# Seeding two score banks with ScalarE copies of the negated maxima, in place of a fourth product with ones

## The reference, cut to what matters

```
q = jnp.einsum('bnd,hde->bhne', query, Wq) * scale
k = jnp.einsum('bmd,hde->bhme', query, Wk)
v = jnp.einsum('bmd,hde->bhme', query, Wv)
logits = jnp.einsum('bhne,bhme->bhnm', q, k)
attn = jax.nn.softmax(logits, axis=-1)
out = jnp.einsum('bhnm,bhme->bnhe', attn, v)
...
return jnp.dot(out, Wp) + bp
```

## Time and profile before

| what | value |
|---|---|
| time, median of 3 runs | 1872.64 us (1872.44 to 1873.9) |
| span of the profiled execution, first to last instruction | 1867.0 us |
| median of the runs less that span | 5.6 us |
| PE busy | 1829.2 us, 98% |
| POOL busy | 1339.4 us, 72% |
| DVE busy | 1216.5 us, 65% |
| ACT busy | 856.0 us, 46% |

### The profile page before, as it was taken

One profiled execution on the slowest core, in us unless ns is written; L12 is line 12 of the kernel. 1 busy time (PEld: TensorE's weight loads), 2 busy tenths in 40 slices (PEclk: granted clock), 3 DMA queues, 4 the chain that ended last, 5 costly groups with the idle time before them and its releaser, 6 DMA issues.

```text
span 1867.0 us, 30732 instructions
## 1 busy us (share of the span) xinstructions
PE 1829.2 (98%) x11400; PEld 1163.7 (62%) x11400; DVE 1216.5 (65%) x2155; ACT 856.0 (46%) x1098; POOL 1339.4 (72%) x711
## 2 busy tenths in 40 slices
PE   7999999999999999999999999999999999999998
PEld 5555555555665555556666565556665555598887
DVE  6666666666666657766666657766666668765565
ACT  3444444444435443443345544443444534475775
POOL 2798778788767867788677767887668787652664
PEclk9999999999999999999999999999999999999999
DMA  4300000002211000022211000022111011453431
GB/s 118 128 24 18 24 18 24 18 24 85 91 46 46 24 18 24 21 81 87 70 45 42 18 7 24 24 80 65 50 39 42 18 35 35 125 159 106 161 136 35
DMA packets 132142, 104.24 MB, mean 56 GB/s; under 512 B 58140, under 2 KB 118684, under 8 KB 130972
## 3 DMA queue, kind: packets, MB, share of 16 engines
q1 hardware_dynamic: 128924, 93.81, 16.8%
q0 software_dynamic: 3072, 8.46, 1.3%
HBM read 69.15 MB, written 29.43 MB: 53 GB/s over the span
## 4 chain that ended last, share of the span: by engine, by line
PE 87%; DVE 4%; POOL 4%; issue 2%; ACT 2%; DMA 1%; SPq 0%; POOLq 0%; DVEq 0%; ACTq 0%
PE score_ps L1161 23%; PE av_ps L1177 23%; PE spare_ps L1123 9%; PE spare_ps L1139 8%; PE spare_ps L1116 4%; PE y_ps L1749 4%; PE spare_ps L441 4%; PE h_ps L1720 4%; PE spare_ps L1188 3%; POOL prob_sum L1037 3%; DVE max_of L1328 1%; PE spare_ps L490 1%; PE spare_ps L465 1%; PE score_ps L1123 0%; PE y_ps L441 0%
## 5 line engine op out<-in xcount | busy, mean ns | idle before, releaser
L1037 POOL TENSOR_TENSOR prob_sum<-prob_sum,probs 128x1024 f32<-128x1024 f32 (+1 forms) x384 | 907.3, 2363 | 196.7 <-ACT probs L1272 164.7
L1328 DVE TENSOR_REDUCE max_of<-spare_ps 128x1 f32<-128x512 f32 x1024 | 656.9, 683 | 336.1 <-PE spare_ps L1139 325.7
L1272 ACT ACTIVATE probs<-score_ps 128x1024 f32<-128x1024 f32 x512 | 502.6, 1026 | 664.4 <-PE score_ps L1161 653.0
L1177 PE MATMUL av_ps<-probs,v 128*64 128x512 f32 x2048 | 487.9, 602 | 2.2 <-ACT probs L1272 1.4
L1177 PEld LDWEIGHTS av_ps<-probs,v 128*64 128x64 f32 x2048 | 129.8, 136 | 240.3 <-issue 218.3
L1033 POOL TENSOR_TENSOR prob_sum<-probs 128x1024 f32<-128x1024 f32 (+1 forms) x64 | 150.4, 2350 | 144.2 <-ACT probs L1272 144.0
L1139 PE MATMUL spare_ps<-k_hi,q_hi 64*128 64x512 f32 x1024 | 227.9, 439 | 11.5 <-DVE max_of L1328 10.6
L1139 PEld LDWEIGHTS spare_ps<-k_hi,q_hi 64*128 64x128 f32 x1024 | 98.1, 184 | 213.1 <-issue 176.9
L1161 PE MATMUL score_ps<-q_hi,k_hi 64*128 64x512 f32 x1024 | 209.0, 403 | 0.2 <-ACT probs L1272 0.2
L1161 PE MATMUL score_ps<-shift_rows,ones 64*128 64x512 f32 x1024 | 203.5, 392 | 0.0
L1161 PE MATMUL score_ps<-q_lo,k_hi 64*128 64x512 f32 x1024 | 202.7, 391 | 0.0
(11 more groups left out here) (278 smaller groups left out, 2367.7 us busy)
## 6 DMA issues: line engine op xcount, KB each, us to landing
o_transposed<-o_out SPq DMA_DIRECT2D x64, 256.0 KB, 2.0
v<-in_L_ffn_W_dram SPq DMA_DIRECT2D x16, 1024.0 KB, 5.6
o_in<-o_transposed SPq DMA_DIRECT2D x28, 512.0 KB, 4.1
w_raw<-in_L_attn_Wq_dram SPq DMA_DIRECT2D x64, 64.0 KB, 2.3
w_raw<-in_L_attn_Wk_dram SPq DMA_DIRECT2D x64, 64.0 KB, 2.2
wv_raw<-in_L_attn_Wv_dram SPq DMA_DIRECT2D x32, 128.0 KB, 3.0
shift_rows<-neg_rows SPq DMA_DIRECT2D x256, 1.0 KB
x<-in_x_dram SPq DMA_DIRECT2D x4, 1024.0 KB, 5.9
```

What stands on the lines that cost most here:

```text
L1037: pool.tensor_tensor(out, out, probs[:, n % RING, heads], ALU.add).then_inc(prob_added, 1)
L1177: last = pe.matmul(av_ps[hd * E:(hd + 1) * E, :], v[:, quad % 2, kt, 2 * first_head + hd, :], probs[:, n % RING, hd, :], start=(kt == 0), ...
L1272: act.activation(probs[:, n % RING], score_ps[n % 2][:, :, :], ACT.Exp).then_inc(probs_ready, 1)
L1328: dve.tensor_reduce(max_of[:, u % 2, kh, j, hd:hd + 1], bank[:, :], AX.X, ALU.max).then_inc(pass_read, 1)
```

## The change

The fourth product goes for all scores but the first two. In its place ScalarE writes -max, as a full 128 x 1024 tile, into the score buffer before the score (the step "seed"), and the three products of q and k add to what stands there: their first matmul no longer starts a new sum. To have -max on all 128 partitions, SyncE moves it to a small tensor in DRAM (`shift_dram`) with four transfers, and then reads it back with one transfer of 512 KB that repeats it on every partition (`spread_shift` into `shift_all`, two buffers). Space for that comes from `o_out`: the normalised output is now written over `sums`, and `turn_sum` waits until the store of the unit before has landed. In the order of steps "seed seed" stands behind each pair of scores, scores now always come in pairs, and in the second line one av moved from the end to the middle.

```
-    "early av av av pass score score pass sum av recip pass score score pass late bite bite",
-    "bite norm score pass early av pass score score pass score pass late av av av",
-    "av pass score score pass early av sum pass score score pass bite late av recip av",
-    "pass norm score score pass early bite bite av pass score score pass late av av av"))
+    "early av av av pass score score seed seed pass sum av recip pass score score seed seed pass late bite bite",
+    "bite norm pass score score seed seed pass early av av pass score score seed seed pass late av av",
+    "av pass score score seed seed pass early av sum pass score score seed seed pass bite late av recip av",
+    "pass norm score score seed seed pass early bite bite av pass score score seed seed pass late av av av"))
...
+            if name == "seed" and h < HALVES and KT * u + kt + 2 < KT * UNITS:
+                yield "seed", KT * u + kt + 2
...
             def move_shift(u):
                 sp.wait_ge(max_done, u + 1)
-                wait(sp, score_ready, KT * (u - 1))
+                wait(sp, shift_in[u % 2], 16 * (u // 2))
                 for r in range(P // BLOCK):
                     rows = neg_rows[r * BLOCK:r * BLOCK + 2 * JT, :]
-                    heads = shift_rows[0:E + 1:E, u % 2, :].rearrange("h (j r i) -> h r j i", j=JT, i=BLOCK)
-                    sp.dma_start(heads[:, r].bitcast(F32), rows.bitcast(F32)).then_inc(shift_in[u % 2], 16)
+                    heads = shift_dram[u % 2].rearrange("h (j r i) -> h r j i", j=JT, i=BLOCK)
+                    sp.dma_start(heads[:, r], rows.bitcast(F32)).then_inc(shift_out, 16)
+
+            def spread_shift(u):
+                sp.wait_ge(shift_out, 64 * (u + 1))
+                wait(sp, seeded, KT * (u - 1) - 2)
+                sp.dma_start(shift_all[:, u % 2], shift_dram[u % 2].rearrange("(a h) n -> a h n", a=1)
+                             .broadcast_to([P, 2, BANK])).then_inc(shift_in[u % 2], 16)
...
-                wait(pe, probs_ready, n - 1)
+                products = [(k_hi[:, par, keys], q_hi[:, par, tokens]), (k_hi[:, par, keys], q_lo[:, par, tokens]),
+                            (k_lo[:, par, keys], q_hi[:, par, tokens])]
                 if n < 2:
+                    pe.wait_ge(first_shift, 64)
...
+                    products.append((one_rows[:, :], shift_rows))
+                else:
+                    pe.wait_ge(seeded, n - 1)
...
+                        last = pe.matmul(score_ps[n % 2][:, hd, :], a[rows], b[rows], start=(n < 2 and i == 0),
+                                         stop=(i == len(products) - 1), skip_group_check=n > 1)
...
+            def seed(n):
+
+                u, kt = divmod(n, KT)
+                if kt == 0 or n == 2:
+                    act.wait_ge(shift_in[u % 2], 16 * (u // 2 + 1))
+                act.wait_ge(probs_ready, n - 1)
+                act.activation(score_ps[n % 2][:, :, :], shift_all[:, u % 2], ACT.Copy).then_inc(seeded, 1)
...
             def turn_sum(u):
                 bank, = spare(("sum", u))
                 dve.wait_ge(sum_ready, u + 1)
-                wait(dve, o_done, u)
+                wait(dve, o_stored[(u - 1) % 2], 16 * ((u + 1) // 2))
                 dve.transpose(sums[:, :], bank[:, :]).then_inc(sum_turned, 1)
...
             def normalise(u):
                 dve.wait_ge(av_ready, KT * (u + 1))
                 dve.wait_ge(recip_spread, u + 1)
-                wait(dve, o_stored[u % 2], 16 * (u // 2))
-                dve.tensor_tensor(o_out[:, u % 2, :], av_ps[:, :], sums[:, :], ALU.mult).then_inc(o_done, 1)
+                dve.tensor_tensor(sums[:, :], av_ps[:, :], sums[:, :], ALU.mult).then_inc(o_done, 1)
```

More of the change, by code:

```diff
@@ L816, in build_attention @@
         neg_rows = sb("neg_rows", [P, BLOCK], F32R)
-        shift_rows = sb("shift_rows", [P, 2, BANK], F32R)
+        shift_all = sb("shift_all", [P, 2, 2, BANK])
+        shift_rows = route.o_hi[:, :, :].rearrange("p c n -> p (c n)")[:, 0:BANK]
         score_ps = [ctx.enter_context(nc.psum_tensor(f"score_ps{i}", [P, 2, BANK], F32)) for i in range(2)]
@@ L856, in build_attention @@
         max_found = sem("max_found")
+        first_shift = sem("first_shift")
+        shift_out = sem("shift_out")
         shift_in = [sem(f"shift_in{i}") for i in range(2)]
+        seeded = sem("seeded")
         score_ready = sem("score_ready")
@@ L905, in load_wv, with move_first_shift @@
                                  ).then_inc(wv_loaded, 16)
+            def move_first_shift():
+                sp.wait_ge(max_done, 1)
+                for r in range(P // BLOCK):
+                    rows = neg_rows[r * BLOCK:r * BLOCK + 2 * JT, :]
+                    heads = shift_rows[0:E + 1:E, :].rearrange("h (j r i) -> h r j i", j=JT, i=BLOCK)
+                    sp.dma_start(heads[:, r].bitcast(F32), rows.bitcast(F32)).then_inc(first_shift, 16)
             def move_shift(u):
                 sp.wait_ge(max_done, u + 1)
-                wait(sp, score_ready, KT * (u - 1))
+                wait(sp, shift_in[u % 2], 16 * (u // 2))
                 for r in range(P // BLOCK):
                     rows = neg_rows[r * BLOCK:r * BLOCK + 2 * JT, :]
-                    heads = shift_rows[0:E + 1:E, u % 2, :].rearrange("h (j r i) -> h r j i", j=JT, i=BLOCK)
-                    sp.dma_start(heads[:, r].bitcast(F32), rows.bitcast(F32)).then_inc(shift_in[u % 2], 16)
+                    heads = shift_dram[u % 2].rearrange("h (j r i) -> h r j i", j=JT, i=BLOCK)
[5 more added lines that the diff above has]
+                             .broadcast_to([P, 2, BANK])).then_inc(shift_in[u % 2], 16)
             def store_o(u):
@@ L917, in store_o @@
                 b, hp, c = u // (2 * PER_BATCH), u // 2 % PER_BATCH, u % 2
-                sp.dma_start(oT_dram[b, hp, :, c * BANK:(c + 1) * BANK], o_out[:, u % 2, :]
+                sp.dma_start(oT_dram[b, hp, :, c * BANK:(c + 1) * BANK], sums[:, :]
                              ).then_inc(o_stored[u % 2], 16)
@@ L951, in _ @@
             sp.wait_ge(rows_set, 2)
+            move_first_shift()
             move_shift(0)
+            spread_shift(0)
             for h in range(HALVES):
@@ L979, in _ @@
                     move_shift(u + 1)
+                    spread_shift(u + 1)
                 if h == 1:
@@ L1047, in _ @@
             pool.memset(prob_sum[:, 0, 0, 0:P], 1.0).then_inc(rows_zeroed, 1)
-            pool.memset(o_out[:, :, :], 0.0).then_inc(rows_zeroed, 1)
+            pool.memset(sums[:, :], 0.0).then_inc(rows_zeroed, 1)
             pool.wait_ge(rows_zeroed, 2)
             pool.tensor_copy(one_rows[:, :], prob_sum[:, 0, 0, 0:P]).then_inc(rows_set, 1)
-            pool.tensor_copy(shift_rows[:, :, :], o_out[:, :, :]).then_inc(rows_set, 1)
+            pool.tensor_copy(shift_rows, sums[:, :]).then_inc(rows_set, 1)
             pool.wait_ge(rows_set, 2)
@@ L1155, in score @@
                     pe.wait_ge(rows_set, 2)
-                products = ((k_hi[:, par, keys], q_hi[:, par, tokens]), (k_hi[:, par, keys], q_lo[:, par, tokens]),
-                            (k_lo[:, par, keys], q_hi[:, par, tokens]), (one_rows[:, :], shift_rows[:, u % 2, :]))
+                    products.append((one_rows[:, :], shift_rows))
+                else:
+                    pe.wait_ge(seeded, n - 1)
                 for i, (a, b) in enumerate(products):
@@ L1160, in score @@
                         rows = slice(hd * E, (hd + 1) * E)
-                        last = pe.matmul(score_ps[n % 2][:, hd, :], a[rows], b[rows],
-                                         start=(i == 0), stop=(i == len(products) - 1))
+                        last = pe.matmul(score_ps[n % 2][:, hd, :], a[rows], b[rows], start=(n < 2 and i == 0),
+                                         stop=(i == len(products) - 1), skip_group_check=n > 1)
                 last.then_inc(score_ready, 1)
@@ L1286, in _ @@
                     exp(*at)
+                if name == "seed":
+                    seed(*at)
                 if name == "wp":
@@ L1336, in read_pass @@
                     dve.wait_ge(max_found, u + 1)
-                    wait(dve, shift_in[(u - 1) % 2], 64 * ((u + 1) // 2))
+                    wait(dve, first_shift, 64 if u > 0 else 0)
+                    wait(dve, shift_out, 64 * u)
                     dve.transpose(neg_rows[:, :].bitcast(F32), neg_max[:, :].bitcast(F32)).then_inc(max_done, 1)
```

7 lines of the change are left out of this document (3 added, 4 removed).

## The result

The changed kernel takes 1840.3 us (1838.4 to 1841.4) against 1873.3 us (1872.4 to 1875.7) for the kernel before on the same chip: ratio 0.983, 95% interval 0.982 to 0.984. So 33 us are saved where 64 were forecast, and the time lies inside the range.

What follows compares the result with a forecast made beforehand. TensorE, busy 98% of the span, was taken to bound nearly every stretch of attention. 117 - 13 - 22 - 10 - 5 - 3 = 64 us saved gave 1808 us against a median of 1872.6, range 1775 to 1842.

Steps and rivals of the forecast that it cites:

- The price of 0.23 us for a product: TensorE's scores: a fourth product of two heads costs 0.23 us; 510 scores losing one save 117 us.
- The duration of a seed and its overlap: ScalarE: a seed takes 0.93 to 1.06 us; 0.93 behind another, 1.05 to its end.
- the order and VectorE: TensorE's passes wait for VectorE's maxima, as they come 0.46 us sooner behind each pair: 5 us more lost.
- The 3 for the ends: Maxima of the last two units late against their scores, and first seeds after two transfers in a row: 3 us lost.
- stalls of scores on seeds: TensorE's second scores wait for seeds in short gaps, and the q bite's pass for q_hi: 32 x 0.4 = 13 us lost.
- route work: ScalarE's norms and table loads stand behind seeds and delay four places in each of three sequences: 10 us lost, an estimate.
- 0.45 us late in each even unit: k bites' high parts behind seeds free the second bank at 6.6 us; the pass ahead of the scores wants it at 6.1.
- The 22 us: Even units: TensorE's sum waits for GpSimd's unbroken adds and weight split, 16.8 us; with bank losses in 12 units, 22 us lost.
- (b): Rival: ScalarE's chain heavier, seeds 1.06 us without overlap, three short gaps of four halves stall; 38 us more, about 1845; 14%.
- (a): Rival: full gain, with short seeds and GpSimd's chain shrinking; 100 us or more kept, about 1765; 6%.
- (c): Rival: repeated read of -max lands late, ScalarE held at a unit's first seed; 128 us of stall, about 1935; 7%.
- (d): Rival: TensorE's new idle time of some 60 us brings a 1.2 GHz clock for stretches; within the range; 2%.

Runs made afterwards that it cites:

- half adds: GpSimd adds the first head only, second head's sums left out, in four kernels: before 1858.3 us, changed 1811.1, without seeds 1762.0, seeds behind bites 1800.7.
- seeds behind bites: Changed kernel with three lines of steps reordered: where bites follow a pair of scores, one or both seeds stand behind a bite; 1824.9 us.
- without seeds: Changed kernel, its order and transfers kept, seeds removed: scores from the third on are three products alone, maxima left out; 1808.3 us.
- the order of before without the fourth product: Kernel before, in its own order, fourth product left out with nothing in its place, so maxima are left out of the exponentials; 1799.2 us.
- the late split: Changed kernel with GpSimd's weight split moved one half later, from an even unit's second half to the odd unit's first; 1835.0 us.

## Where the prediction was right and where it was wrong

**What held.** The price of 0.23 us for a product: a step where nothing waits falls by 0.45 us for two scores (7.80 to 7.35), and with seeds and half of GpSimd's adds out of the way 96 us are saved between like kernels (1858.3 to 1762.0). The duration of a seed and its overlap (two in 1.98 us). The hidden transfers. The list of places: scores for seeds, sum for GpSimd, pass for VectorE. The sum's wait of 28.7 us in 22 waits is a little above "15 to 25 us over some 20 waits". That the time lies in the range is the width of the range, 25 to 95 us saved, and no merit of the sum: only half of the 64 us came.

**The account.** From 1872.4 us on: half adds 14.1 less; product and seeds gone, new order, 96.3 less; adds whole again 46.3 more; seeds 32.0 more. That is 1840.3. Against 117 us, 20.7 are lost to the new order with VectorE's part, 32.2 to GpSimd (46.3 less the 14.1 which it held already), 32.0 to the seeds: 85, where the prediction had 53. In its own terms: 32 for seeds where it had 13 and 10, 32 for GpSimd where it had 22, 21 for the order and VectorE where it had 5. That is the order of taking them apart; in another, GpSimd gets 15 and the seeds 49. The 3 for the ends have no run of their own. The premise that TensorE alone bounded the kernel before was off too: with half adds it is 14.1 us faster.

**The step that failed first: what stands behind a seed.** The prediction charged 13 us for stalls of scores on seeds and 10 for route work. It followed the high parts of the k bites and of the q bite in the third line, each only up to its own bank. It did not follow them into VectorE's list, where a late q_hi holds q_lo, the inverse and the maxima, nor did it look at the fourth line's two bites. This is 0.77 us in each plain four halves and 15 us in all by the run with seeds behind bites. In units with route work `o_hi` and `o_lo` come in between too, and one pass waits 3.71 us in the changed kernel's timeline:

```profile
429.22 0.60 ACT L1282 ACTIVATE q_hi<-spare_ps 128x512 fp32r<-128x512 f32 x1
...
429.70 1.07 ACT L332 ACTIVATE o_hi<-o_in 128x1024 fp32r<-128x1024 f32 x1
...
430.80 3.04 DVE L513 TENSOR_TENSOR o_lo<-o_in,o_hi 128x1024 fp32r<-128x1024 f32 x1 [0.26 <-ACT o_hi L332]
...
435.47 0.50 PE L1160 MATMUL spare_ps<-k_hi,q_hi 64*128 64x512 f32 x2 [3.71 <-DVE max_of L1361]
```

In the kernel with seeds behind bites this pass waits 3.8 us, so that edit doesn't mend it. The five other waits of this kind in the changed kernel, 2.2 to 2.5 us, can't be put on the seeds: without seeds there are five of 2.4 to 2.5. With half adds and no seeds the longest wait for maxima is 1.0. Of the wait for q_hi, 21.9 us are there without seeds too, and 43.3 with.

**The second: the late bank.** "0.45 us late in each even unit" is not made by seeds ahead of the high parts: the step from the pair ahead of the bites to the next one takes 7.0 us in the new order with seeds and without. It takes 6.56 in the order of before without the fourth product, but there it holds one pass less, 0.23 us. The stretch up to the odd unit's first pair holds the same work in both orders. In the kernel before with half adds, and then without seeds and with half adds:

```profile
368.86 0.40 PE L1161 MATMUL score_ps<-q_hi,k_hi 64*128 64x512 f32 x2
...
385.66 0.39 PE L1161 MATMUL score_ps<-q_hi,k_hi 64*128 64x512 f32 x2
```

```profile
346.18 0.40 PE L1184 MATMUL score_ps<-q_hi,k_hi 64*128 64x512 f32 x2
...
361.91 0.40 PE L1184 MATMUL score_ps<-q_hi,k_hi 64*128 64x512 f32 x2
```

16.80 us less six products would be 15.42; it takes 15.73. So 0.3 us are lost in each plain even unit. The place fits the pass directly behind the bites, which in the changed kernel starts at 410.94 us, 0.15 after the second k bite's low part ends; no run moves that pass alone. I charged the loss in 12 units alone, since GpSimd's chain was to cover it elsewhere. It doesn't: the four last adds wait for the exponential of the pair that stands behind the late pass. 32 units of 0.3 are 10 us of the 20.7, an estimate.

**The third: GpSimd.** The 22 us lie between the 15 and the 32 measured. The model (a row of work without a pause from the first half on) was wrong for plain units, as the late split showed, and right where tokens are sent.

**The rivals.** The time is near that of (b), about 1845, and its sign "score waits exceed 30 us" (34.3) came, yet its mechanism (seeds with no overlap, three stalls in four halves) did not occur: in the plain stretch TensorE waits 0.41 us for seeds twice in four halves, and only one of the two lengthens a step, by 0.24 us (5.03 against 4.79 without seeds). Its sentence that all four operations of a pair lie in one chain was the right warning. (a) fell: only without seeds and with half adds is the time near it (1762.0). (c) fell. (d) came in part: the slices show full clock, but four stretches at 1.2 GHz against one are about 5 us, an estimate from 1.5 us each.

**What stays open.** How the 20.7 us divide beyond the late bank, how much of the 46.3 is VectorE's shorter `o_lo`, and what part the clock has in each difference. An order that beats the seeds behind bites was not found; that version, at 1824.9 us, is the fastest here that computes all.

## What to carry to other kernels

Work taken from a busy engine is worth its price only up to the next engine's list: here a kernel with the product simply gone keeps 74 of 117 us. That one run tells early what a replacement can be worth, as long as the other engines' lists stay as they are. When an instruction is put into another engine's list, follow what it delays through the lists of the third and fourth engine until the first waits again; such a loss carried no wait on the new instruction in any view here. Losses found one by one neither add nor can be mended one by one: a wait removed gives others their room back, or takes it. And look at the clock of short stretches behind long waits, since 40 slices hide them.

## What the hardware showed unexpectedly

A ScalarE copy of 128 x 1024 from SBUF into PSUM takes 1.03 us, like the exponential from PSUM to SBUF (1.02) and nearly like a copy within SBUF (1.06): the PSUM target gives 0.03 us. Half the size takes 0.61. Products that add to a bank filled by ScalarE run at the step of 0.23 us, as the rest. Behind a wait of 3.71 us TensorE ran at 1.2 GHz for some 3 us. VectorE's subtraction of two SBUF tiles takes 2.24 us on average beside GpSimd's whole adds and 1.24 beside half adds, while the maxima, read from PSUM, stay at 0.68 in both.
